# Scaling the residual's rows on ScalarE instead of VectorE, with a new order of calls, in a four-layer linear-attention and experts kernel

## The reference, cut to what matters

```python
mod = (silu(c) @ wmod).reshape(16, 6, 1, 128)         # per sequence: sa, ca, ga, sb, cb, gb
x = L0_attn_x_in
h = layernorm(x) * (1 + ca) + sa
h = sqrt(128) * h + pos_emb
for i in range(4):                                     # encoder layers
    n = layernorm(h, ln1_s[i], ln1_b[i])
    q, k, v = n @ Wq[i] + bq[i], n @ Wk[i] + bk[i], n @ Wv[i] + bv[i]
    qp, kp = elu(q) + 1, elu(k) + 1                    # 16 heads of 8
    att = qp @ (kp.T @ v) / (qp @ kp.sum(0) + 1e-6)    # per head
    h = h + att @ Wo[i] + bo[i]
    n = layernorm(h, ln2_s[i], ln2_b[i])
    h = h + relu(n @ W1[i] + b1[i]) @ W2[i] + b2[i]    # 512 wide
h = layernorm(h, lnf_s, lnf_b)
x = x + ga * h
t = layernorm(x) * (1 + cb) + sb
x = x + gb * (top-2 of 8 experts, gated, 64 wide, by the router's softmax, + a shared expert, 128 wide)
```

## Time and profile before

| | us |
|---|---|
| median of 3 runs | 575.06 |
| the runs | 571.92, 575.22, 575.06 |
| profiled execution | 572.23 |
| its span, first to last instruction | 570.3 |
| PE busy | 553.8 (97%) |
| DVE busy | 440.9 (77%) |
| ACT busy | 395.6 (69%) |
| POOL busy | 261.1 (46%) |

### The profile page before, as it was taken

How to read it: one execution, slowest core, us unless ns; L and a number is a source line. 1 busy time by engine, 2 the same in 40 slices (tenths; PEclk the granted TensorE clock), 3 DMA queues, 4 the chain that set the end, 5 groups by cost and what they waited for, 6 DMA issues and landing times.

```text
span 570.3 us, 13221 instructions
## 1 busy us (share of the span) xinstructions
PE 553.8 (97%) x4572; PEld 531.6 (93%) x4572; DVE 440.9 (77%) x1545; ACT 395.6 (69%) x1395; POOL 261.1 (46%) x431
## 2 busy tenths in 40 slices
PE   5899999999999999999999999999999999999997
PEld 3588899999999999998999999998999999999997
DVE  5977677788986777777997777778897667667896
ACT  3977978786766766786585766787676666766652
POOL 4335668564323446654503536646313435335420
PEclk9999999999999999999999999999999999999999
DMA  7700345000000000000000000000000000000000
GB/s 228 225 2 1 103 154 185 2 1 2 20 10 11 1 2 2 1 2 2 2 20 20 1 2 1 1 2 1 2 20 20 2 2 1 2 2 1 2 20 18
DMA packets 11065, 15.60 MB, mean 27 GB/s; under 512 B 976, under 2 KB 8240, under 8 KB 10616
## 3 DMA queue, kind: packets, MB, share of 16 engines
q1 hardware_dynamic: 8920, 12.54, 6.9%
q0 software_dynamic: 448, 1.25, 0.8%
q10 hardware_dynamic: 1632, 0.98, 0.6%
HBM read 12.63 MB, written 2.14 MB: 26 GB/s over the span
## 4 chain that ended last, share of the span: by engine, by line
PE 85%; ACT 7%; DVE 5%; POOL 1%; issue 1%; ACTq 1%; DVEq 0%; POOLq 0%
PE psA L1643 20%; PE psB L1643 19%; PE psD L1643 19%; PE psC L1643 18%; PE psC L1715 2%; PE psB L1715 1%; PE psD L1715 1%; PE psA L1715 1%; ACT L529 1%; ACT L483 1%; PE psA L1766 1%; PE psB L1766 1%; ACT H L498 1%; PE psC L1766 0%; ACT xC L463 0%
## 5 line engine op out<-in xcount | busy, mean ns | idle before, releaser
L848 POOL TENSOR_TENSOR rstdD<-msD,neghalf 128x2 f32<-128x2 f32 x20 | 14.0, 699 | 53.8 <-ACT ziD L475 41.7
L1643 PE MATMUL psC<-w,H 128*128 128x128 f32 x256 | 34.2, 276 | 0.5 <-ACT H L498 0.5
L1643 PE MATMUL psB<-w,H 128*128 128x128 f32 x256 | 33.1, 275 | 0.0
L1643 PE MATMUL psA<-w,H 128*128 128x128 f32 x256 | 33.0, 275 | 0.0
L1643 PEld LDWEIGHTS psC<-w,H 128*128 128x128 f32 x256 | 31.1, 192 | 1.5 <-ACT H L498 1.5
L1643 PE MATMUL psD<-w,H 128*128 128x128 f32 x256 | 31.8, 275 | 0.0
L1643 PEld LDWEIGHTS psB<-w,H 128*128 128x128 f32 x256 | 30.9, 192 | 0.0
L1643 PEld LDWEIGHTS psA<-w,H 128*128 128x128 f32 x256 | 30.8, 192 | 0.0
L1643 PEld LDWEIGHTS psD<-w,H 128*128 128x128 f32 x256 | 30.3, 192 | 0.0
L475 ACT ACTIVATE eqkA<-xA 128x129 f32<-128x129 f32 x64 | 19.3, 307 | 11.3 <-DVE xA L1195 10.5
L848 POOL TENSOR_TENSOR rstdA<-msA,neghalf 128x2 f32<-128x2 f32 x20 | 14.6, 731 | 26.2 <-ACT eqkA L475 23.0
(11 more groups left out here) (589 smaller groups left out, 2401.1 us busy)
## 6 DMA issues: line engine op xcount, KB each, us to landing
M<-modulation_rows SPq DMA_DIRECT2D x2, 1280.0 KB, 9.2
M<-modulation_rows SPq DMA_DIRECT2D x1, 2560.0 KB, 8.8
out<-X SPq DMA_DIRECT2D x15, 128.0 KB, 1.8
M<-in_attn_W SPq DMA_DIRECT2D x3, 256.0 KB, 3.1
X<-in_attn_x_in ACTq DMA_DIRECT2D x2, 256.0 KB, 3.6
M<-in_attn_W ACTq DMA_DIRECT2D x1, 256.0 KB, 3.6
wo<-in_attn_Wo POOLq DMA_DIRECT2D x1, 256.0 KB, 4.7
wm<-in_wmod SPq DMA_DIRECT2D x1, 256.0 KB, 4.2
```

Of the source, the lines that this page charges most:

```text
L848: pool.tensor_tensor(b.rstd[:, :], b.ms[:, :], neghalf[:, :], ALU.pow).then_inc(b.s_rstd.sem, 1)
L1643: return pe.matmul(o, lhsT, rhs, start=start, stop=stop)
```

## The change

ACT takes over the scaling for odd n: two activations, one for each tile, with the inverse deviation as a scale per partition. DVE's function goes. PE, ACT, DVE and POOL get new orders of the same calls; no other function is changed. `ENTRY_PE` gives the order in which PE makes the first rows.

```diff
-ENTRY_PE = (3, 1, 2, 0)
+ENTRY_PE = (0, 1, 3, 2)
...
+            def scale(b, i, n):
+
+                act.wait_ge(b.s_rstd.sem, b.s_rstd.value(i, n))
+                for t in range(TILES):
+                    last = act.activation(b.xn[:, t, 0:D - 1], x(b, i)[:, t, 1:D], ACT.Identity, scale=b.rstd[:, t:t + 1])
+                last.then_inc(b.s_normed.sem, 1)
+
...
-            def scale(b, i, n):
-
-                dve.wait_ge(b.s_rstd.sem, b.s_rstd.value(i, n))
-                dve.tensor_tensor(b.xn[:, :, 0:D - 1], x(b, i)[:, :, 1:D],
-                                  b.rstd[:, :].unsqueeze(2).to_broadcast([P, TILES, D - 1]), ALU.mult)\
-                    .then_inc(b.s_normed.sem, 1)
-
```

ACT, the entry (`scale` stands behind `less_wo_means(0)`; D's exponentials come later):

```diff
             centre(B, 0)
+            squares(B, 0, 1)
             bias_rows(1)
+            less_wo_means(0)
+            scale(B, 0, 1)
+            scale(A, 0, 1)
+            high(1)
+            transposed(B, 0, 0)
             transposed(A, 0, 0)
-            squares(B, 0, 1)
+            bias_high(1)
+            key_exps(B, 0, 0)
             key_exps(A, 0, 0)
             query_exps(A, 0, 0)
-            less_wo_means(0)
-            high(1)
-            transposed(B, 0, 0)
+            centre(D_, 0)
+            query_exps(B, 0, 0)
+            squares(D_, 0, 1)
             centre(C, 0)
-            bias_high(1)
-            key_exps(B, 0, 0)
+            scale(D_, 0, 1)
+            att_transposed(A, 0, 0)
             squares(C, 0, 1)
```

PE, the entry:

```diff
             bias_rows(1)
+            fold_weights(1)
+            transposes(B, 0, 0)
             transposes(A, 0, 0)
-            fold_weights(1)
+            project_keys(B, 0, 0)
+            project_queries(B, 0, 0)
             project_keys(A, 0, 0)
             project_queries(A, 0, 0)
-            transposes(B, 0, 0)
             sums(A, 0, 0)
+            sums(B, 0, 0)
             attend(A, 0, 0)
-            project_keys(B, 0, 0)
+            attend(B, 0, 0)
             out_project(A, 0, 0)
+            transposes(D_, 0, 0)
+            out_project(B, 0, 0)
             fold_weights(2)
             out_project2(A, 0, 0)
```

PE, the end of the last layer and the experts of C and D:

```diff
                 out_project(D_, i, 3)
+                logits(A, i)
                 transposes(C, i, 7)
                 out_project2(D_, i, 3)
-                logits(A, i)
                 expand(C, i, 3, 0)
                 expand(C, i, 3, 1)
-                transposes(D_, i, 7)
                 contract(C, i, 3, 0)
                 logits2(A, i)
                 gate(A, i, 2)
+                transposes(D_, i, 7)
...
+                coef_transposes(C, i)
+                spread(D_, i, 0)
+                gate(D_, i, 1)
```

```diff
                 squares(A, i, 3)
                 relu(B, i, 0, 0)
+                scale(A, i, 3)
                 relu(B, i, 0, 1)
...
+                    squares(A, i + 1, 1)
                     squares(B, i + 1, 1)
+                    scale(A, i + 1, 1)
+                    scale(B, i + 1, 1)
                 tokensT(D_, i)
```

More of the change, by code:

```diff
@@ L603, in _ @@
                 if i == 0:
-                    less_w2_means(1)
                     high(6)
+                scale(C, i, 3)
+                squares(A, i, 4)
                 transposed(C, i, 2)
-                squares(A, i, 4)
                 att_transposed(B, i, 1)
+                transposed(A, i, 3)
+                squares(D_, i, 3)
                 key_exps(C, i, 1)
-                squares(D_, i, 3)
-                transposed(A, i, 3)
-                query_exps(C, i, 1)
                 squares(B, i, 4)
+                scale(D_, i, 3)
                 if i == 0:
                     high(7)
+                relu(A, i, 1, 0)
+                if i == 0:
                     less_wo_means(2)
-                relu(A, i, 1, 0)
+                query_exps(C, i, 1)
                 relu(A, i, 1, 1)
+                transposed(B, i, 3)
                 transposed(D_, i, 2)
@@ L626, in _ @@
                 query_exps(D_, i, 1)
+                att_transposed(C, i, 1)
+                scale(A, i, 5)
                 relu(B, i, 1, 0)
+                transposed(A, i, 4)
                 relu(B, i, 1, 1)
                 squares(C, i, 4)
-                transposed(A, i, 4)
-                transposed(C, i, 3)
                 key_exps(A, i, 2)
                 att_transposed(D_, i, 1)
+                transposed(C, i, 3)
+                if i == 0:
+                    experts_high()
+                squares(D_, i, 4)
                 relu(C, i, 1, 0)
@@ L637, in _ @@
                 query_exps(A, i, 2)
-                squares(D_, i, 4)
-                transposed(D_, i, 3)
+                scale(B, i, 5)
                 transposed(B, i, 4)
                 squares(C, i, 5)
-                if i == 0:
-                    experts_high()
+                transposed(D_, i, 3)
                 key_exps(B, i, 2)
+                query_exps(B, i, 2)
+                scale(C, i, 5)
                 att_transposed(A, i, 2)
-                query_exps(B, i, 2)
                 relu(D_, i, 1, 0)
@@ L769, in _ @@
                     att_transposed(A, i + 1, 0)
+                    squares(D_, i + 1, 1)
+                    scale(C, i + 1, 1)
+                    scale(D_, i + 1, 1)
                     squares(A, i + 1, 2)
+                    att_transposed(B, i + 1, 0)
+                    transposed(D_, i + 1, 0)
                     transposed(A, i + 1, 1)
-                    transposed(D_, i + 1, 0)
-                    att_transposed(B, i + 1, 0)
+                    transposed(C, i + 1, 0)
+                    key_exps(C, i + 1, 0)
                     key_exps(D_, i + 1, 0)
-                    transposed(C, i + 1, 0)
         @block.gpsimd
@@ L925, in _ @@
                 rstd(A, i, 5)
+                add_bias(D_, i, 3)
                 rstd(C, i, 4)
@@ L1483, in _ @@
                 move(B, i, 5)
-                scale(D_, i, 5)
-                positive_queries(C, i, 2)
                 masked(C, i, 2)
+                move(A, i, 6)
                 low_part(D_, i, 4)
-                move(A, i, 6)
                 divided(C, i, 2)
@@ L1531, in _ @@
                     in_enter(C, i + 1)
+                move(B, i, 7)
                 masked(C, i, 3)
@@ L1727, in project_keys @@
                 pe.wait_ge(b.s_xT.sem, b.s_xT.value(i, 2 * l + 1))
+                if i > 0 and l == 0:
+                    pe.wait_ge(b.s_mod.sem, b.s_mod.value(i - 1, 2))
                 if i == 0:
@@ L2169, in _ @@
                 if i + 1 < STEPS:
+                    out_project(A, i + 1, 0)
+                spread(D_, i, 1)
+                down(D_, i, 0)
+                if i + 1 < STEPS:
                     out_project2(A, i + 1, 0)
-                down(D_, i, 0)
+                    out_project(B, i + 1, 0)
                 down(D_, i, 1)
+                if i + 1 < STEPS:
+                    transposes(D_, i + 1, 0)
                 down(C, i, 0)
```

554 lines of the change are left out of this document (261 added, 293 removed).

## The result

The changed kernel takes 577.21 us in the median of 9 runs; the kernel before takes 573.19 in the 9 runs beside it. The ratio is 1.0064, 95% interval 1.0045 to 1.0083: some 3.7 us slower. One run of 1406.63 us is left out of the ratio. The profiled execution took 576.5 us (span 574.7), against 572.23 and 570.3 before. The time lies in the range of the forecast, but the forecast of no change did not hold: the loss is small and real.

The account below looks back on a forecast made before the run. TensorE was taken to bound from 40 us to the last experts, chains of the other engines before. Terms summed to +0.1 us, 575.2 on the median; forecast between two run groups 574.5 us, no change, 8-in-10 range 570.0 to 580.0.

Parts of the forecast that it names:

- The entry: First 40 us: B's and A's scaled rows come later, B's second expansion half at 43.4 us; +1.0 us, bounds -4 and +4.
- Step 0: Where the weights are folded and ScalarE has least to spare: calls coming late cost 0.5 us, bounds 0 and 3.
- The last layer's end: Waits for C's power and a relu, with shorter gaps, shrink by 0.5 us a step: -2.0 us, bounds 0 and 4.
- changes of format: On TensorE, fp32r follows fp32 178 times instead of 174: +0.4 us.
- The longer chain: From a layer's last contraction to the next transposes: 0.1 us wait at three tight leads a step, +1.2 us, bounds 0 and 6.0.
- The pair's length: Two overlapping ScalarE scaling activations take 0.69 us, bounds 0.4 and 0.79.
- The experts: A table load ahead of gate and up no longer delays TensorE in three steps: -0.8 us; the last step's 0.8 wait stays.
- Steps of 133.1 us: Sign of the forecast: steps between the same calls take 133.1 us, before 133.6 and 133.4.
- rival 1: Longer chain decides, at transposes behind contractions and ScalarE in step 0: 7.3 us more, 582; chance 0.16.
- Rival 2: The entry gains, with paired chains and its 1.3 us wait gone: -4 instead of +1, time 568.5; chance 0.13.
- Rival 3: The clock stays down longer in the entry as TensorE waits more there: +2.2 us, 576.7; chance 0.10.
- Rival 4: VectorE, slowed by something shared with GpSimd, gains less than 29.8 us; time stays inside the forecast, no separate chance.

Follow-up runs that it names:

- e8: The changed kernel with each ScalarE scaling of 128x127 split into two pieces of 64 and 63 columns: 590.97 us, ratio 1.0320.
- e6: The changed kernel with experts_high waiting for five of seven weight transfers, the down matrix's two counting on another semaphore: 576.43 us, ratio 1.0058.
- e2: The kernel before with only experts_high moved ahead of C's relu of layer 1 in ScalarE's list: 576.10 us, ratio 1.0039.
- e11: The changed kernel with SyncE starting step 0's table rows only after the seven experts' weight transfers have landed: 575.28 us, ratio 1.0033.
- e5: The changed kernel with experts_high moved behind C's squares of index 6 in ScalarE's list: 575.22 us, ratio 1.0033.
- e9: e5 plus two swaps: B's shift ahead of its gate on GpSimd, C's transposed rows ahead of B's squares on ScalarE: 573.84 us, ratio 1.0012.
- e12: e10 with C's relu ahead of D's squares for index 8 in ScalarE's list: 573.65 us, ratio 1.0000.
- e13: e12 with A's row copies also ahead of D's squares for index 8, and B's last deviation ahead of D's on GpSimd: 576.19 us, ratio 1.0044.
- e10: e9 with VectorE making the low part of C's rows of index 7 ahead of D's move: 575.47 us, ratio 1.0037.

## Why the prediction was right or wrong

**The time was close, the verdict wrong.** Forecast +0.1 us on the profiled execution, measured +4.3. That 577.21 lies in the range is in part luck: the forecast of 574.5 leaned on a median of three runs, 575.06, where nine runs of the same kernel gave 573.19, so its base was too high by nearly half of the loss that it missed. By the table of lags:

- *The entry*, forecast +1.0 (transposes of B at 19.05 and A at 19.65, output projection's transposes of A at 27.7, B's second half of the expansion at 43.4). Measured 19.28, 19.86, 28.03 and 42.76, and 0.4 us behind; eight profiles of this entry order under other labels (without e8, which changes it) are 0.6 to 1.6 behind, the mean of all nine 1.0. Right, in size and in the walk. The one profile of the changed kernel was an early one there, and its 576.5 us lie 0.7 below the median of the runs. e6 came out 1.0 us later, and that delay stayed.
- *Step 0, "0.5 for calls that come late there (bounds 0 and 3)"*: this is the step that failed. Measured +3.0 between 45 and 75 us of work, just at the upper bound, and 2.3 of it by one call that the text doesn't mention. I counted what ScalarE has to do in step 0 (74.6 us of 90.8 and 7 to 8 more) and took idle time as a cover. But an engine's list is served in order. `experts_high` waits for a landing that the new order did not bring forward (79.1 us before, 79.9 after), and the diff shows the call moved forward by eight calls. The busy share said nothing about it; the row of the kernel before that does is ScalarE's start of that call at 82.88, 3.7 us behind the landing, which I had not read. e2 and e11 show the wait to be the cause: moved there alone, the call slows the old kernel, and with the landing ahead of it the place costs next to nothing. The price is 2 us in the old kernel (e2, at equal work) and 2.0 in the new one (e5, e11).
- *The last layer's end, -2.0 (bounds 0 and 4)*: the second that failed. The waits of the earlier trace rows did go. In their place came two others of 0.57 and 0.80 us a step (excess over the pace), together 1.4, as much as the 1.3 before. I looked for the waits that the new order removes and not for who is late next. After 75 us of work the terms add up to -1.8 (without the 0.4 for changes of format, which the table counts as work), measured +1.2; e9's and e12's swaps give 1.4 to 1.6 us back.
- *The longer chain, +1.2 (bounds 0 and 6.0)*: hidden. Behind the entry the profile shows no wait of TensorE for rows that ScalarE scaled. The term was too high, but e8 shows how near the edge it is: 0.34 us more a call cost 13.8.
- *The pair's length*, 0.69 us, was right to the row:

```profile
170.25 0.68 ACT L453 ACTIVATE xnC<-xC,rstdC 128x127 f32<-128x127 f32 x2
```

- *The experts, -0.8*: the table load is out of the way in the first three steps, as forecast, and the wait in the last step stays (0.82 at 560.87, forecast 0.8).
- *Steps of 133.1 us*: measured 133.7 from 136.16 to 269.86 us, between the same calls. The sign for rival 1 was 135; the 0.6 above the forecast have the other cause above.

**The rivals.** Rival 1 (a chain through ScalarE and ScalarE itself in step 0) had the right engine and, in step 0, the right stage. Its mechanism in the steps does not show in this order; e8, with pairs that are longer yet, loses 13.8 us, by the chain or by ScalarE's fuller list. Rival 2 didn't happen; the wait of 1.3 us in the entry went, as it said, and others came. Rival 3, a longer stretch at the low clock, did not happen in this profile:

```profile
22.00:23.00 1.00, 1.00 (x8) 1.00 (x7) 1.00 (x2) 1.00 (x1) 0.00 (x0) 0.62 1.06 305
```

The stretch at a lower granted clock of the earlier trace rows has moved from 26 to 31 us to the first transposes and projections, 19.3 to 22.7 us, behind the wait of 1.0 us for B's rows. It did not become longer here, but in e12 and e13, with the same entry, it did (last section). Rival 4 holds in a small part: on VectorE 2.7 of the 29.8 us came back as longer calls.

**What stays open:** 0.7 us of the loss in step 0 ahead of the wait, which arises between 45 and 65 us of work; whether e8's loss is the chain or ScalarE's fuller list; and why the same entry ends 0.4 to 1.6 us late.

## What to carry to other kernels

When a change re-orders the lists of in-order engines, go through the diff for every call with a wait on a transfer, however small, and compare where the engine will reach it with when the transfer lands; a busy share of 80% covers work, not a wait at the head of the list. When a wait is taken off the path, look up who is late next before booking the gain: here two waits of 0.3 to 0.6 us stood right behind, and each of the four kernels with further swaps showed another. When two executions are compared by a start time, subtract first how late each one already was: e6's start at 79.82 us misled me. And a wait can be mended at the other end: delaying 1.3 MB that nobody needed yet gave as much as moving the call.

## What was unexpected of the hardware

- The seven transfers took 9.2 to 9.6 us from issue to landing beside 2.6 MB of table rows, and 5.9 to 6.4 us beside half of it. They landed in the order of their issue and about as far apart: in the changed kernel issued from 66.7 to 70.3 us, landed from 76.2 to 79.9.
- An activation on 128x64 takes 336 ns, one on 128x127 some 400 and one on 128x1280 1.27 us. Halves save a sixth each: two small ones cost more than the one they replace by 0.17 us of busy time.
- Some of VectorE's calls on 128x128 that read only SBUF are long beside one kind of work of GpSimd. In the changed kernel 17 calls of lines 1141, 1151 and 1169 took 684 to 801 ns; all 17 ran beside one of GpSimd's additions of 128x256 (lines 869 and 895). Calls of the same lines without such an addition beside them took 335 to 353 ns. The moves (line 1226), which read PSUM, kept 333 to 354 ns beside them too. In the kernel before, 13 calls were long in the same way. That the two engines share something there was not tried. One such pair, where the second product of the two started at 222.35 us and took 801 ns:

```profile
222.09 1.06 DVE L1141 SCALAR_TENSOR_TENSOR ziA<-X,in_mvA,M 128x128 f32<-128x128 f32 x2
222.31 0.69 POOL L895 TENSOR_TENSOR xC<-xC,bo_all 128x256 f32<-128x256 f32 x1 [1.35 <-ACT xnC L453]
```

- An fp32 product of sums, attend or contract leaves two records of 0.11 us each (two products, x4; four, x8), a transposition of 128x128 one (two, x2), so "pass twice" in the text ahead of the prediction is shown for the products and not for the transposes.
- The same order of the entry came out 0.4 to 1.6 us behind in nine profiles, and the granted clock differs among them. From 22 to 29 us it is 0.95 in the changed kernel; e10 and e12 in this stretch:

```profile
22.00:29.00 7.00, 4.91 (x34) 3.85 (x32) 6.28 (x20) 6.91 (x27) 1.73 (x3) 1.00 0.49 142
22.00:29.00 7.00, 6.36 (x30) 5.94 (x28) 5.19 (x16) 6.92 (x25) 1.81 (x3) 0.52 0.53 150
```

At 0.50, which is 1.2 of 2.4 GHz, the fp32r products start 0.21 us apart, at full clock 0.12. e12 and e13, with 0.52 in this stretch, are the two latest out of the entry. But e10, with 1.00 all through the entry's projections, is not the earliest, so the clock is not all of the difference. What decides where and whether the low stretch falls was not tried.
